# Two graph and mixture-of-experts layers on one core: a chunk's eight row scatters issued two steps apart instead of together

## What is computed

```python
def moe0(x):                       # 8 private experts of 512, top 2, plus a shared one
    rw = softmax(x @ Wr); topw, topi = top_k(rw, 2); topw /= topw.sum()
    return shared(x) + sum(topw[e] * (gelu(x @ W1p[e] + b1p[e]) @ W2p[e] + b2p[e]) for e in topi)

x = x + 0.9 * rownorm(A * (y @ y.T)) @ layernorm(x) + 0.1 * h0
x = x + moe0(layernorm(x))
n = layernorm(x)
x = x + concat(n, A @ n, einsum('ij,ji->i', A, A)) @ weight + bias
x = x + moe1(layernorm(x))         # 8 experts of 256, top 2, softmax weights
```

## Time and profile before

| | us |
|---|---|
| median of three executions | 1472.78 |
| lowest and highest of them | 1468.39, 1475.87 |
| span of the profiled execution | 1555.4 |
| TensorE busy in it | 1367.5 (88%) |
| VectorE busy | 929.2 (60%) |
| ScalarE busy | 649.6 (42%) |
| GpSimd busy | 461.5 (30%) |

### The profile page before, as it was taken

The page is one execution under the profiler, slowest core; times in us unless marked ns, Lnnn a source line. Parts: engine busy times, 40 slices in busy tenths (PEclk is TensorE's granted clock), DMA queues, the critical chain, the costliest instruction groups (busy, mean ns, idle before and its releaser), DMA issues.

```text
span 1555.4 us, 21717 instructions
## 1 busy us (share of the span) xinstructions
PE 1367.5 (88%) x6536; PEld 829.7 (53%) x6536; DVE 929.2 (60%) x2670; ACT 649.6 (42%) x1108; POOL 461.5 (30%) x450
## 2 busy tenths in 40 slices
PE   5998999999999999998689999999999998766771
PEld 2443444444444444456578877466666666545550
DVE  6775858576776767684322224777777777432224
ACT  3454344343444433444244344565555555422220
POOL 2102021111202020213545554223323332465652
PEclk9999999999999999999899999999999999978885
DMA  9688988696888787875366442889888888433435
GB/s 314 253 335 315 337 297 305 239 341 238 321 274 317 265 318 266 304 248 206 104 250 223 170 165 96 312 296 311 296 292 308 304 287 250 117 111 113 126 109 202
DMA packets 117360, 386.22 MB, mean 248 GB/s; under 512 B 20116, under 2 KB 49587, under 8 KB 87824
## 3 DMA queue, kind: packets, MB, share of 16 engines
q1 hardware_dynamic: 77296, 327.32, 60.9%
q10 hardware_dynamic: 27136, 33.93, 6.2%
q0 software_dynamic: 12832, 23.81, 4.3%
HBM read 332.80 MB, written 57.41 MB: 251 GB/s over the span
## 4 chain that ended last, share of the span: by engine, by line
PE 51%; issue 12%; DVE 10%; another core or an unknown queue 5%; ACT 4%; POOL 3%; DMA 2%; DVEq 0%; POOLq 0%; ACTq 0%; SPq 0%
PE agg L742 14%; PE d L846 7%; PE s L726 6%; PE d L790 4%; POOL rows_scratch L1798 3%; PE d L800 2%; PE d L680 2%; DVE adj_over_wb L386 2%; PE agg L913 2%; PE u L831 2%; PE u L833 2%; ACT h L1101 2%; PE u L827 1%; PE u L832 1%
## 5 line engine op out<-in xcount | busy, mean ns | idle before, releaser
L742 PE MATMUL agg<-m,xn 128*128 128x512 f32 (+1 forms) x800 | 399.4, 585 | 0.0
L1065 ACT ACTIVATE mabs<-m 128x512 f32<-128x512 f32 (+1 forms) x400 | 243.7, 619 | 322.4 <-DVE m L1561 289.4
L1561 DVE TENSOR_TENSOR m<-s,ring 128x512 f32<-128x512 f32 (+1 forms) x400 | 268.2, 676 | 184.2 <-PE s L726 127.7
L726 PE MATMUL s<-ymov,ysta 128*128 128x512 f32 (+1 forms) x400 | 244.8, 616 | 42.7 <-DVE m L1561 24.7
L1798 POOL DMA_INDIRECT rows_scratch<-xrow,idx x160 | 183.8, 1149 | 297.8 <-DVE xrow L1306 102.8
L1807 POOL DMA_INDIRECT y_scratch<-yo,ids x164 | 160.9, 981 | 138.9 <-DVE yo L1456 70.8
L742 PEld LDWEIGHTS agg<-m,xn 128*128 128x128 f32 x800 | 152.2, 191 | 62.8 <-issue 41.9
L726 PEld LDWEIGHTS s<-ymov,ysta 128*128 128x128 f32 x400 | 75.3, 190 | 199.7 <-issue 97.8
L386 DVE TENSOR_TENSOR adj_over_wb<-ring,adj_over_wb 128x512 fp32r<-128x512 f32 (+1 forms) x216 | 138.8, 672 | 48.5 <-ACT adj_over_wb L1165 44.7
L1784 POOL TENSOR_TENSOR rstd<-vareps,mhalf 128x4 f32<-128x4 f32 x30 | 38.3, 1277 | 405.6 <-DVE vareps L1218 405.6
L1165 ACT CAST adj_over_wb<-ring 128x512 fp32r<-128x512 f32 (+1 forms) x216 | 125.6, 607 | 45.7 <-PE agg L920 42.6
(11 more groups left out here) (242 smaller groups left out, 1982.8 us busy)
## 6 DMA issues: line engine op xcount, KB each, us to landing
ring<-in_adj_in SPq DMA_DIRECT2D x180, 1024.0 KB
ring<-in_adj_out SPq DMA_DIRECT2D x30, 1024.0 KB
wb<-blob_scratch SPq DMA_DIRECT2D x27, 834.0 KB
rows_scratch<-yo ACTq DMA_DIRECT2D x81, 260.0 KB, 6.7
stage<-in_adj_out SPq DMA_DIRECT2D x19, 1024.0 KB
ring<-in_adj_in SPq DMA_DIRECT2D x20, 784.0 KB
xt<-rows_scratch SPq DMA_DIRECT2D x54, 260.0 KB
wbz<-blob_scratch SPq DMA_DIRECT2D x27, 193.0 KB
```

The source lines that it names most:

```text
L726: pe.matmul(sbank[s % 2][:, 0:n], ysta[:, s * P:(s + 1) * P], ymov[:, k % 2, 0:n], start=True, stop=True).then_inc(s_made, 1)
L742: pe.matmul(abank[:, 0:n], xn[:, b, :], m[:, b % M_BUFS, 0:n], start=b == 0, stop=b == NB - 1).then_inc(S["agg_blocks"], 1)
L1065: act.activation(mabs[:, b % ABS_BUFS, 0:width(k)], m[:, b % M_BUFS, 0:width(k)], ACT.Abs).then_inc(abs_made, 1)
L1561: dve.tensor_tensor(m[:, s % M_BUFS, 0:width(k)], sbank[s % 2][:, 0:width(k)], slot_part(LOAD_AT[k, l, False][0], s % LB, width(k)), ALU.m ...
```

## The change

Two tables give each of a chunk's eight scatters a step of its own. In loop A six go at steps 29, 31, 33, 35, 37 and 39 and two at steps 1 and 3 of the next iteration, each behind a wait for the mask product of that step. In loop Z three go at steps 36, 38 and 40 and five at steps 1, 3, 5, 7 and 9 of the next iteration, each behind a wait for TensorE's products. In the last iteration of each loop, chunk 9's own eight stay together as before, and what is left of chunk 8's goes out at its steps without waits.

```diff
+A_SPREAD = ((29, 31, 33, 35, 37, 39), (1, 3))
+Z_SPREAD = ((36, 38, 40), (1, 3, 5, 7, 9))
...
-                if mid and A_AT["scatter"] <= s < A_AT["scatter"] + 2 * TB:
+                if k == CH and A_AT["scatter"] <= s < A_AT["scatter"] + 2 * TB:
                     scatter_rows(0, k - 1, s - A_AT["scatter"])
+                if mid and k < CH and s in A_SPREAD[0]:
+                    pool.wait_ge(m_made, k * NB + s)
+                    scatter_rows(0, k - 1, A_SPREAD[0].index(s))
+                if k >= 2 and s in A_SPREAD[1]:
+                    if k < CH:
+                        pool.wait_ge(m_made, k * NB + s)
+                    scatter_rows(0, k - 2, len(A_SPREAD[0]) + A_SPREAD[1].index(s))
...
-                if mid and s == at["scatter"]:
+                last = isinstance(k, int) and k == CH
+                if last and s == at["scatter"]:
                     for i in range(2 * TB):
                         scatter_rows(1, CH + k - 1, i)
+                if mid and not last and s in Z_SPREAD[0]:
+                    wait(pool, SZ["agg_blocks"], k * NB + s - LAG)
+                    carry(pool, pool_carried)
+                    scatter_rows(1, CH + k - 1, Z_SPREAD[0].index(s))
+                if s in Z_SPREAD[1] and not (isinstance(k, int) and k < 2):
+                    if not last:
+                        wait(pool, SZ["agg_blocks"], k * NB + s)
+                        carry(pool, pool_carried)
+                    scatter_rows(1, CH + k - 2, len(Z_SPREAD[0]) + Z_SPREAD[1].index(s))
```

## The result

The changed kernel takes 1481.51 us (median of six, 1478.66 to 1487.97), the one before 1472.32 in its six on the same chip (1468.39 to 1475.87): ratio 1.0074, 95% interval 1.0056 to 1.0092, so slower by 8 to 14 us. The forecast was 1483 out of 0 us for loop A, +4 for loop Z and +7 for the last chunk.

The account below looks back on a forecast made before the run. TensorE, busy 88% of the span, was taken to bound both loops. Loop A 0, loop Z +4 and the last chunk +7 made +11 us on 1472.8, giving 1483, range 1463 to 1493.

Parts of the forecast that it names:

- Loop A, 0: Spreading loop A's scatters of chunks 0 to 8 costs nothing and saves nothing: 0 us, bounds 0 and 12.4 us saved.
- Rivals 1 and 2: Loop A's TensorE pauses are real and go: all, -12.4 us, chance 0.20; half, -6 us, chance 0.17.
- Loop Z, +4: Loop Z, chunks 0 to 7: later last scatters lengthen the norm's waits on VectorE, +4 us, bounds -3 and +12.
- The norm's wait grows by at most 1.3 us: Loop Z: the last scatter starts 1.3 us later, so each of 8 chunks' norms waits at most that much more.
- The lower bound of the term: Loop Z: -3 us if a less crowded queue lands in 5 us instead of 7.2 and all 4.7 us go.
- The last chunk, +7: Last iteration of loop Z: scatters behind power and tile 27 make the norm 10 us late; GpSimd's queue passes on +7.
- The upper bound, 11 us: Last chunk: +11 us if TensorE's and VectorE's whole delay passes on.
- Rival 3: Last chunk's queue doesn't pass on because late tiles wait for something else: +4 from loop Z alone, 1477, chance 0.10.
- Rival 4: Loop Z pays in full, +12, with +7 to +11 for the last chunk: 1492 to 1496, chance 0.08.
- the lock rule: Loop Z: a spaced scatter holding the shared SBUF port blocks VectorE's splits, up to 38 us; 1500 given 3 in 100.

Follow-up runs that it names:

- the mended one: The changed kernel, but in loop Z's last iteration chunk 8's five remaining scatters go out together at step 1, ahead of the power: 1471.07 us, ratio 1.0001.

## Why the prediction was right in size and wrong in parts

- **Loop A, 0: right.** The ratio is 1.0008 for loop A's spread alone (0.9993 to 1.0023). Its waits on GpSimd have nothing behind them that is late, and the pauses were no price at all. Rivals 1 and 2 fall with them. The reason given, that 82.6 us of the profiled execution are not in the runs, was the right reading; a second profile would have made it certain.
- **Loop Z, +4: wrong, it is 0.** The step that failed is "The norm's wait grows by at most 1.3 us", which carried the landing of 7.2 us over unchanged. The last scatter did start 1.2 us later, but landed 5.7 us or less after its start, and the norm's waits did not grow: 2.8 to 4.2 us over the loop in three undisturbed profiles with the spread, 3.3 to 5.7 in five without it. The lower bound of the term had the shorter landing (5 us), though not that it only makes up for the later start. The same shows between undisturbed profiles: wherever the norm waits for it in loop Z, the eighth scatter lands 6.0 to 7.4 us after its start in the kernel before (four times) and 3.5 to 5.6 in the mended one (six times). Counted from the chunk's copy the landing stayed where it was, as the table above shows, so the later start took only from the time in flight; a queue made less crowded by the seven before it, as the bound had it, is not needed for that.
- **The last chunk, +7: mechanism right, size wrong.** It is 10.5 us by itself. The norm is 9.2 us late (forecast 10), GpSimd waits 4.89 us for tile 28 (4.9), and the two scatters more take 2.6 us (2.5). Missing were the waits for tiles 29 and 30 (3.4 us); the other 1.1 is the rest in the table above. The upper bound, 11 us for the whole delay, is what came. That GpSimd's queue sets the end was right too, but was taken from a profile in which that queue stood a fifth of the time. Rival 3, that late tiles hide it, falls.
- **Rival 4, loop Z in full, and the lock rule.** In this version neither came: with both spreads and the last chunk mended the ratio is 1.0001. The Trainium skill's rule that one of VectorE and GpSimd blocks the other (SBUF — State Buffer, "SBUF: two separate sides") gives no 38 us here. But the rival's idea, a norm waiting for its landing in every chunk, is real and two steps away; its price was put far too low, for TensorE's stand and its clock were left out.
- The forecast came within 2 us of the measured time partly by luck: 4 us too much in loop Z and 3.5 too little in the last chunk nearly cancelled. Without the experiments 1483 would have looked like a confirmed sum.

No version here beats both kernels. The mended one equals the kernel before.

## What to carry to other kernels

When work moves from one iteration to the next, follow it into the last iteration, whose order is another: there two instructions behind four others cost all of this change's loss, and what bounds that stretch may be an engine that is busy only a third of the span. If a profile's span doesn't match the runs, profile the same kernel again before pricing anything from it. A landing that isn't waited for can be two microseconds from being the most expensive wait in the loop, so know the slack before spreading anything towards it.

## What was not expected of the hardware

- One profiled execution of an unchanged kernel took 1555.4 us and another 1471.9, with 2.2% less TensorE busy time (1367.5 and 1337.1 us) and a mean granted clock of 0.978 instead of 0.964 in the second. The first had pauses of 3 us at places where no other profile has one.
- A row scatter's landing differed by its place: in loop Z 6.0 to 7.4 us after its start in the kernel before, 3.5 to 5.7 when spread, 5.3 to 7.2 when spread but 2 us later, and 2.6 in the last chunk, when the adjacency loads are over. Its packets move in bursts 3 to 5 us apart, so in loop Z its landing went by the burst that it caught and hardly by its start. GpSimd's own row, 0.96 to 1.4 us, shows none of this.
- A wait of some 4 us on TensorE in each chunk cost the waits and then 10 to 14 us more over loop Z, in products that ran longer at the lower granted clock.
